# Local attention stream: transposes of the probabilities, and ScalarE's copy of them, issued ahead of the second half of the turns of queries and keys

## The reference

```python
def attn_layer(x, Wqkv, qs, ksc, Wo):          # x: (8, 256, 128), 16 heads of 64
    q, k, v = jnp.split(x @ Wqkv, 3, -1)
    q, k = l2norm(q) * qs, l2norm(k) * ksc
    q, k = rotary(q), rotary(k)
    out = local_attention(q, k, v)             # windows of 32: each looks at itself and the one before
    return out @ Wo
def ffn_layer(x, g, bln, W1, b1, W2, b2):
    a, gate = jnp.split(norm(x) @ W1 + b1, 2, -1)
    return a * gelu(gate) @ W2 + b2
for i in range(6):
    x = attn_layer(shift_tokens(x), ...) + x
    x = ffn_layer(shift_tokens(x), ...) + x
```

## Time and profile before

| | us |
|---|---|
| median of 3 runs | 4067.25 (4065.52 to 4068.03) |
| the profiled execution | 4065.2 |
| its span from first to last instruction | 4063.4 |
| PE busy | 3725.1 (92%) |
| ACT busy | 3267.2 (80%) |
| DVE busy | 3158.2 (78%) |
| POOL busy | 2616.4 (64%) |

### The profile page before, as it was taken

How to read it: one execution, slowest core, us unless ns; L and a number is a source line. 1 busy time by engine, 2 the same in 40 slices (tenths; PEclk the granted TensorE clock), 3 DMA queues, 4 the chain that set the end, 5 groups by cost and what they waited for, 6 DMA issues and landing times. The chain is left out here.

```text
span 4063.4 us, 167180 instructions
## 1 busy us (share of the span) xinstructions
PE 3725.1 (92%) x66080; PEld 2910.6 (72%) x66080; DVE 3158.2 (78%) x6474; ACT 3267.2 (80%) x10760; POOL 2616.4 (64%) x2490
## 2 busy tenths in 40 slices
PE   8969979999999999999986978999999999999996
PEld 7948957777777777777774547777777777777773
DVE  2242268988888888888875879888888889888883
ACT  4434459999999999999983768999999999999994
POOL 0010047777877778777862658787777877778771
PEclk9979989999999999999997989999999999999997
DMA  1000024333333333333420013333333333333331
GB/s 40 19 1 25 18 75 123 100 107 119 106 117 106 105 120 96 111 119 104 122 86 8 1 36 112 115 109 118 99 111 115 110 115 102 107 116 106 117 107 32
DMA packets 547030, 361.35 MB, mean 89 GB/s; under 512 B 32321, under 2 KB 532817, under 8 KB 546001
## 3 DMA queue, kind: packets, MB, share of 16 engines
q1 hardware_dynamic: 546256, 350.66, 28.7%
HBM read 248.59 MB, written 101.97 MB: 86 GB/s over the span
## 5 line engine op out<-in xcount | busy, mean ns | idle before, releaser
L1341 POOL TENSOR_TENSOR lt_t<-lt_t,lt_rn 128x512 f32<-128x512 f32 x768 | 786.2, 1045 | 664.6 <-DVE lt_rn L1195 662.7
L1071 ACT ACTIVATE lt_pb<-lt_pb,lt_mx 128x64 f32<-128x64 f32 x3072 | 1022.5, 342 | 0.0
L1335 POOL TENSOR_TENSOR lt_t<-lt_t 128x512 f32<-128x512 f32 x768 | 972.0, 1288 | 2.6 <-DVE lt_t L1169 2.6
L49 PE MATMUL ps<-lt_wh,lt_xh 128*128 128x512 f32 (+1 forms) x1536 | 577.7, 376 | 44.1 <-DVE lt_t L1169 26.0
L1071 ACT ACTIVATION_READ_ACCUMULATOR lt_pb<-lt_pb,lt_mx 128x1 f32 x3072 | 598.8, 195 | 0.0
L1051 ACT ACTIVATE lt_qkT<-ps 128x512 f32<-128x512 f32 x768 | 459.4, 598 | 129.7 <-PE ps L871 129.2
L1180 DVE TENSOR_REDUCE lt_ss<-lt_sq 128x8 f32<-128x512 f32 x768 | 520.3, 677 | 41.7 <-ACT lt_sq L1046 36.0
L1169 DVE TENSOR_TENSOR lt_t<-ps,lt_tab 128x512 f32<-128x512 f32 x768 | 526.0, 685 | 4.0 <-issue 1.1
L1175 DVE TENSOR_TENSOR lt_t<-ps,lt_tab 128x512 f32<-128x512 f32 x768 | 522.4, 680 | 1.6 <-PE ps L871 0.3
L50 PE MATMUL ps<-lt_wl,lt_xh 128*128 128x512 f32 (+1 forms) x1536 | 519.4, 338 | 1.4 <-issue 1.4
L51 PE MATMUL ps<-lt_wh,lt_xl 128*128 128x512 f32 (+1 forms) x1536 | 520.5, 339 | 0.0
(11 more groups left out here) (230 smaller groups left out, 7468.0 us busy)
## 6 DMA issues: line engine op xcount, KB each, us to landing
lt_vw<-v_scratch SPq DMA_DIRECT2D x768, 256.0 KB, 3.7
v_scratch<-lt_vv SPq DMA_DIRECT2D x384, 256.0 KB, 2.1
lt_wraw<-in_lt_wqkv SPq DMA_DIRECT2D x56, 384.0 KB, 6.2
moe_w<-in_moe_w SPq DMA_DIRECT2D x32, 256.0 KB, 2.9
lt_wo<-in_lt_wo SPq DMA_DIRECT2D x48, 128.0 KB, 4.0
lt_w<-in_lt_w SPq DMA_DIRECT2D x12, 341.0 KB, 4.4
lt_w<-in_lt_w SPq DMA_DIRECT2D x12, 192.0 KB, 4.0
lt_gl<-in_lt_qs SPq DMA_DIRECT2D x2, 768.0 KB, 5.7
```

The source lines that it names most:

```text
L49: nc.tensor.matmul(out, lh, rh, start=start, stop=False)
L1071: ins = nc.scalar.activation(p, p, ACT.Exp, bias=mx[:, par, c:c + 1], accum_out=sm[:, par, c:c + 1])
L1335: nc.gpsimd.tensor_tensor(o, o, t2[:, t, :], ALU.add).then_inc(padd[t], 1)
L1341: nc.gpsimd.tensor_tensor(o, o, rn[:, u[1] % 2, 8 * t:8 * t + 8].unsqueeze(2).to_broadcast([P, 8, DH]), ALU.mult).then_inc(qkd[t], 1)
```

## The change

Two calls are moved, one in PE's list and one in ACT's. Nothing is added or removed, and DVE, POOL and SP keep their lists.

```diff
@@ PE's slot @@
                     c = chunk(L, s, 14)
                     if c:
                         variance(c)
+                    if u4:
+                        turn_weights(u4)
                     if u2:
                         turn(u2, 1)
-                    if u4:
-                        turn_weights(u4)
                     if u5:
                         merge(u5)
@@ ACT's slot @@
                     if u5:
                         take_output(u5)
+                    if u4:
+                        take_weights(u4)
                     if u2:
                         take_turned(u2, 1)
                     c = chunk(L, s, 14)
                     if c:
                         inverse_deviation(c)
-                    if u4:
-                        take_weights(u4)
                     if u3:
                         exponentials(u3, 0)
```

## The result

The changed kernel takes 4146.09 us (median of 4 runs, 4145.21 to 4155.86) against 4067.64 for the kernel before, which ran beside it. The ratio is 1.0201 with a 95% interval of 1.0188 to 1.0214. It is slower by 78 us by the medians and 82 us by the ratio. The mean granted clock of the profiled execution was 0.966, against 0.970 before. That explains little of it: runs of the kernel before at 0.966 and 0.967 took 4066 to 4071 us.

A forecast was written before the change was run, and what follows sets the result against it. PE leads, neither PE nor ACT full, with a two-slot loop through DVE and POOL delaying L911. Regular groups 48.6, groups after a layer's turn 10, layer 0 5.6: 64 us on 4067.25 gives 4131 us, range 4090 to 4150.

The forecast's parts named there:

- What bounds the kernel: PE leads at 92% busy, ACT has 80%, neither is full; L911's data come late from POOL.
- the loop over two slots: From L911 of slot 2 through DVE and POOL to L911 of slot 4: 13.63 us; what stands in it costs time.
- Slot by slot: Regular group of 8 slots: 0.47 us lost in slots 2 and 4, 0.49 in slot 0; 1.43 in all.
- The case where every late slot pays: Rival: POOL's release in slot 3 also moves, so nothing is given back; 1.9 us a group, 4157 us; 8%.
- Slot 0 was lost through ACT: Slot 0: PE has time to give, but ACT's exponentials and then the gelus come later; 0.49 us lost.
- The groups just after a layer's turn: PE's idle time covers slot 2; slot 3 pays 0.47 instead, slot 4 nothing new, slot 0 0.49: about 1.0 us.
- Slots 5 to 7: Data are early, the transposes swap at no cost, the merge covers ACT's copy; failure costs 0.1 or so in three slots.
- Slot 1: L911 fills the 0.46 us gap, but the merge then waits for ACT's copy of the output; gain 0, at most 0.05.
- The inverse deviation in slot 6: It comes 0.49 us later on ACT; DVE reads it a slot later, so 0; at most 0.49 a group.
- Signs named in advance: If right: idle before L871 little or gone, before L911 up 50 to 80 us, slots 0, 2, 4 longer by 0.5.
- One sign of being wrong: Slots 5 to 7 growing, which would mean that the scores wait for ACT's copy of the second turn.
- The page on weight loads: Second turn's weights might load during L911's wait, making the sum about 14 us less; left out of the sum.

The follow-up runs named there:

- short product: Kernel before with POOL multiplying only one of eight pieces of the probabilities (for time alone): 3995.68 us; the same edit of the changed kernel: 4035.72 us.
- split wait: Changed kernel, but the scores wait for ACT's copy of the second turn only before their second half: 4135.78 us, 1.0168.
- ACT's half alone: Kernel before with only ACT's list changed (copy of the probabilities before copy of the second turn), PE's order kept: 4195.57 us, 1.0320.

## Why the prediction was right, and what it mis-sized

- *What bounds the kernel, and the loop over two slots.* Right. Taking the late product away in two ways (shorter, earlier) made the old order 73 and 51 us faster. The 49 us of idle time before L911 understate the wait, which is 66 us from start to start, as worked out above. The short product also takes 0.75 us of work off POOL in each slot, so the 73 us need not be the wait alone.
- *Slot by slot.* The changed kernel with the split wait has these steps without the scores' wait. It is 1.0168, about 68 us over before by the ratio and 72 by the medians; the sum of the prediction was 64. The table shows a step in slots 0, 2 and 4, none in slot 3, and the step moved from slot 2 to 3 after a layer's turn. The case where every late slot pays would have been 90. Slot 0 was lost through ACT, as said: in the middle of a layer ACT's exponentials, the gelus and the end of the slot all move by the same 0.40 us in the two groups where the product is a little late, and by 0.28 to 0.29 in the one where it is most late. The groups just after a layer's turn grew by 1.4 instead of 1.0; half of the difference is slot 5, whose late product was not in the sum.
- *Slots 5 to 7.* This is the term that was mis-sized. The prediction said that ACT's copy of the second turn ends before the merge is through and that the scores are covered. The copy does end where I put it, but the scores start 0.21 us after it, not at once, and that is 0.10 us past the merge. Merge to scores grew from 0.95 to 1.06. The term stood at 0 in the sum; the prediction had priced its failure at "0.1 or so in three slots", and that is what slots 5, 6 and 1 show. Taken away, it brings 7 to 13 us, about half or more of the 15 us between forecast and result. Without it the rest of the sum is 68 to 72 us against 64. That 4146 is inside the range at all is a matter of 4 us.
- *Slot 1.* Right: the filled gap became the merge's wait for ACT's copy of the output, 0.26 us in the slot shown, 12.9 us in all.
- *The inverse deviation in slot 6.* I took 0, and it was 0. DVE's reader (L1236) starts 2.4 us or more after ACT's second instruction of it (L1094) has ended, in all 48 cases of the changed kernel, and its idle time is 1.8 us in all, as before.
- *Signs named in advance.* The idle time before L871 went, as said. That before L911 was to grow by 50 to 80 us and grew by 93.8; no run says how much of the surplus belongs to which slot. One sign of being wrong came true as well, in small: slots 5 to 7 did grow, by 0.01 to 0.09 us in the regular group, and for the reason named there, that the scores wait for the copy of the second turn.
- *The page on weight loads.* By the Trainium skill, "TensorE: Matmul & The Clock Gate", section "Step-by-step: what each phase is for", weight loads may be pulled ahead of matmuls in flight. Here no load ran during the wait: PEld had 0.60 us of idle time before L911's own loads, and the first load of the second turn came 1177.23 - 1177.12 = 0.11 us before its first matmul. In slot 5, with no wait, it was 1184.62 - 1184.51 = 0.11 as well. The step was 0.46 behind the wait and 0.50 without one, and 0.43 in slot 6, where there is no wait either. Leaving the term out was right.

## What to carry to other kernels

A gap in an engine's list can be filled only by work whose inputs are there at that time. Look up when the producer of the moved instruction ends, in every slot of the pattern, before the gap is counted as a gain: here L911 had 49 us of idle time of its own, which was the sign that its data come late even at its old place. A late input is mended at its producer: moving POOL's product in front of an addition that could wait gave 51 us with the old order. And when work is moved behind another engine's copy, the cover needs a margin for the time from the end of that copy to the start of the matmul behind it.

## What the runs showed of the hardware that I had not expected

The time from the end of ACT's copy to the start of the matmul that waits for it depends on which matmul it is. In the changed kernel the scores (L899) start 0.21 us after the end of the copy of the second turn, as the median over all slots, and in the kernel with ACT's half alone it is 0.21 again, though the scores start 0.44 us later there. The second turn (L871) starts 0.14 us after the copy of the first one, in 97 waits of the kernel before. The merge (L943) starts 0.05 us after the copy of the output, in 47 waits of the changed kernel. Behind POOL's product L911 starts after 0.10 to 0.11 us. In PE's list up to five semaphore waits stand before the scores, two before the second turn and one to three before the merge; whether that is the reason was not tried.
